# Keeping the finished tiles of two graph convolutions on chip and storing them behind the pass

## What is computed

```python
def _gcn_conv(x, W, b, src, dst, norm, num_nodes):
    h = x @ W
    msg = norm[:, None] * h[src]
    agg = jax.ops.segment_sum(msg, dst, num_segments=num_nodes)
    return agg + b
...
h = jax.nn.relu(_gcn_conv(x, W1, b1, src2, dst2, norm, N))
h = jax.nn.relu(_gcn_conv(h, W2, b2, src2, dst2, norm, N))
return h @ Wfc + bfc
...
x = _layernorm(x + _L0_gnn_ref(...))
# the start of the attention layer
x = (x - mu) * jax.lax.rsqrt(var + LN_EPS) * ln_gamma + ln_beta
x = x @ W_in + b_in
scores_u = x @ W_u + b_u
scores_v = x @ W_v
```

## Time and profile before

| | |
|---|---|
| median of 3 runs | 7572.42 us (7566.16 to 7602.41) |
| the profiled execution | 7592.25 us, its span 7590.4 us |
| mean granted TensorE clock | 0.769 of full speed |
| busy share of the span | PE 65%, VectorE 62%, ScalarE 42%, POOL 65% |
| DMA | 925.17 MB, mean 122 GB/s |
| pass c1 | gathers from 1327.36 to 2392.48 us, next stage's first gather at 2417.78 |
| pass c2 | gathers from 2417.78 to 3481.83 us, next stage's first gather at 3550.20 |

### The profile page before, as it was taken

One profiled execution on the slowest core, in us unless ns is written; L12 is line 12 of the kernel. 1 busy time (PEld: TensorE's weight loads), 2 busy tenths in 40 slices (PEclk: granted clock), 3 DMA queues, 4 the chain that ended last, 5 costly groups with the idle time before them and its releaser, 6 DMA issues. The chain is left out here.

```text
span 7590.4 us, 94731 instructions
## 1 busy us (share of the span) xinstructions
PE 4935.2 (65%) x26906; PEld 3772.5 (50%) x26906; DVE 4690.6 (62%) x12437; ACT 3186.4 (42%) x7393; POOL 4909.0 (65%) x4968
## 2 busy tenths in 40 slices
PE   8999701667676777774356655856656666777774
PEld 6777601444444555553344544435555543555553
DVE  8999701555554677775456666645666566566666
ACT  0222200444443444441244444735665642555553
POOL 0677775777776777774777773047777700777774
PEclk9767655888887888886566667967777777889887
DMA  1333201222223222223566665557777822666665
GB/s 29 80 81 79 58 2 28 53 56 55 55 55 48 53 55 56 56 56 65 162 179 178 178 178 120 194 189 231 232 224 223 224 66 79 217 211 207 208 211 146
DMA packets 793547, 925.17 MB, mean 122 GB/s; under 512 B 115987, under 2 KB 652059, under 8 KB 786139
## 3 DMA queue, kind: packets, MB, share of 16 engines
q0 software_dynamic: 198144, 441.54, 22.8%
q1 hardware_dynamic: 372654, 365.42, 16.2%
q10 hardware_dynamic: 222252, 112.14, 5.0%
HBM read 724.85 MB, written 193.87 MB: 121 GB/s over the span
## 5 line engine op out<-in xcount | busy, mean ns | idle before, releaser
L757 POOL DMA_INDIRECT arena<-t,d_src x2496 | 2454.7, 983 | 908.2 <-issue 756.2
L796 PE MATMUL ps<-arena 128*128 128x128 f32 (+2 forms) x8320 | 1796.5, 377 | 699.2 <-DMA arena<-t,d_src 616.4
L796 PEld LDWEIGHTS ps<-arena 128*128 128x128 f32 x8320 | 1584.7, 257 | 951.9 <-issue 845.9
L805 DVE TENSOR_TENSOR arena<-arena,ps 128x512 f32 (+2 forms) x1040 | 835.1, 803 | 733.8 <-PE ps L796 661.8
L757 POOL DMA_INDIRECT arena<-t,d_typed x832 | 823.9, 990 | 489.0 <-issue 248.3
L721 POOL DMA_INDIRECT d_rec<-arena x784 | 792.6, 1011 | 441.5 <-issue 250.3
L2749 POOL DMA_INDIRECT arena<-t,s_dst x832 | 797.4, 958 | 296.0 <-issue 249.6
L793 PE MATMUL ps<-int_tmp 128*128 128x512 bf16 (+1 forms) x1664 | 555.3, 402 | 488.1 <-DVE arena L805 305.1
L1973 PE MATMUL ps<-arena 128*128 x2496 | 420.2, 303 | 544.3 <-ACT arena L1869 255.8
L1234 PE MATMUL ps<-arena 128*128 128x416 f16 x3328 | 760.5, 382 | 0.0
L1973 PEld LDWEIGHTS ps<-arena 128*128 128x128 f32 (+1 forms) x2496 | 363.9, 210 | 611.5 <-issue 587.2
(11 more groups left out here) (451 smaller groups left out, 8079.8 us busy)
## 6 DMA issues: line engine op xcount, KB each, us to landing
spill<-arena ACTq DMA_DIRECT2D x104, 1024.0 KB, 7.5
arena<-spill SPq DMA_DIRECT2D x208, 512.0 KB
arena<-d_loT SPq DMA_DIRECT2D x104, 512.0 KB
arena<-s_loT SPq DMA_DIRECT2D x52, 1024.0 KB, 6.0
arena<-key_d SPq DMA_DIRECT2D x98, 512.0 KB
t<-arena SPq DMA_DIRECT2D x49, 1024.0 KB, 4.5
arena<-t,d_src POOLq DMA_INDIRECT x2496
arena<-t,d_typed POOLq DMA_INDIRECT x832
```

The lines of the kernel that those rows point to most:

```text
L757: pool.indirect_dma_start(out=rows[r][:, i, :], out_offset=None, in_=table, in_offset=bass.IndirectOffsetOnAxis(ap=idx[:, 8 * n + i:8 * n ...
L796: return nc.tensor.matmul(self.banks[i // 4][:, bass.ds(self.slot[i], self.width)], weights, rows, start=False, stop=False, skip_group_che ...
L805: nc.vector.tensor_tensor(at, at, got, ALU.add).then_inc(self.added, 1)
```

## The change

In both `sync` functions SP first waits until `added` has reached 204 of 208, and issues all stores behind that. In c2 the features are written into the tile's own columns of `acc_gcn` and the scores into an array of their own behind it, so there is no row block to wait for, and each tile is stored by two DMAs, 512 bytes and 32 bytes a row.

```diff
@@ FirstNodes.sync @@
+                sp.wait_ge(self.sums.added, 2 * HALVES - 4)
                 for t in range(0, DONE):
                     sp.wait_ge(self.out, t + 1)
                     store(t)
@@ SecondNodes.__init__ @@
-                for n in [REST * D] * 7 + [REST * (D + H), NT * H] + [REST * 6] * 2 + [REST * 2] * 2 + [REST] * 6:
+                for n in [REST * D] * 7 + [0, NT * H] + [REST * 6] * 2 + [REST * 2] * 2 + [REST] * 6:
...
-                self.rows = rows.rearrange("p (t f) -> p t f", f=D + H)
+                self.scores = arena[:, AT_ACC + NP:AT_ACC + NP + NT * H]
@@ SecondNodes.feature_rows @@
                 step = Chain(dve, self.y_v, t)
-                need(dve, self.stored, 16 * t)
-                step(nc.vector.tensor_tensor(self.rows[:, 0:w, 0:D], tiled(self.vectors_bank(1, w)), bcast_mid(bias["L1_gnn_b_in"], w), ALU.add))
+                step(nc.vector.tensor_tensor(tiled(of_tiles(acc_gcn, t, w)), tiled(self.vectors_bank(1, w)), bcast_mid(bias["L1_gnn_b_in"], w), ALU.add))
@@ SecondNodes.score_rows @@
-                step(nc.vector.tensor_tensor(self.rows[:, 0:w, D:D + H], uv[:, :, 0:H], bcast_mid(b_u[:, :], w), ALU.add))
+                step(nc.vector.tensor_tensor(tiled(of_tiles(self.scores, t, w, H), H), uv[:, :, 0:H], bcast_mid(b_u[:, :], w), ALU.add))
@@ SecondNodes.sync @@
-                def store(t, i):
+                def store(t):
                     number, = numbers(sp, t, 1)
-                    sp.dma_start(t2[bass.ds(P * number, P), :], self.rows[:, i, :]).then_inc(self.stored, 16)
+                    sp.dma_start(t2[bass.ds(P * number, P), 0:D], of_tiles(acc_gcn, t)).then_inc(self.stored, 16)
+                    sp.dma_start(t2[bass.ds(P * number, P), D:D + H], of_tiles(self.scores, t, 1, H)).then_inc(self.stored, 16)
+                sp.wait_ge(self.sums.added, 2 * HALVES - 4)
                 for t in range(0, DONE):
                     sp.wait_ge(self.rows_rdy, 2 * t + 2)
-                    store(t, 0)
+                    store(t)
                 sp.wait_ge(self.rows_rdy, 2 * DONE + 2)
-                for i in range(REST):
-                    store(DONE + i, i)
+                for t in range(DONE, NT):
+                    store(t)
...
-                sp.wait_ge(self.stored, 16 * NT)
+                sp.wait_ge(self.stored, 32 * NT)
```

More of the change, by code:

```diff
@@ L1331, in __init__ @@
                 assert o <= REP_AT
-                self.A, self.aT, self.hT, self.r, self.z, self.zT, self.xiT, rows, self.v_new = buf[0:9]
-                self.rows = rows.rearrange("p (t f) -> p t f", f=D + H)
+                self.A, self.aT, self.hT, self.r, self.z, self.zT, self.xiT, _, self.v_new = buf[0:9]
+                self.scores = arena[:, AT_ACC + NP:AT_ACC + NP + NT * H]
+                assert AT_ACC + NP + NT * H <= AT_Q
                 self.parts = [a.rearrange("p (t c) -> p t c", c=6) for a in buf[9:11]]
```

## The result

| | before | after |
|---|---|---|
| median of 13 runs | 7576.53 us (7565.63 to 7602.41) | 7590.32 us (7581.34 to 7596.07) |
| ratio, 95% interval | | 1.0018 [1.0011, 1.0025] |
| span of the profiled execution | 7590.4 us | 7588.4 us |
| c1, first gather to c2's first gather | 1090.4 us | 1103.2 us |
| c2, first gather to the next stage's first gather | 1132.4 us | 1138.2 us |

The changed kernel takes 13.8 us more, 0.18%. The two spans alone would say the opposite: the profiled execution of before lies 16 us above its median, and its stages behind c2, which the change does not touch, are 18.4 us longer than in the profile after.

What follows compares the result with a forecast made beforehand. POOL's gather issue was taken to pace both passes, and SP's stores to end c1. Terms -1.0 + 7.7 + 3 + 3.3 + 2.1 gave +15.1 us on the 7572.4 median: 7587.5 us, range 7562 to 7608.

Steps and rivals of the forecast that it cites:

- Stores leaving the pass: Mid-pass: taking the stores out gains nothing, since POOL's own issue sets the pace; 0 us.
- Rival 1: Mid-pass: the stores did slow the gathers, 10.6 ns each, 15.3 us saved in all, total 7572; chance 0.12.
- SP's stream in c1, +7.7: End of c1: 49 stores at 0.823 us each put the last at 2422.4 instead of 2414.67; +7.7 us.
- SP held by its queue, +3: End of c1: from about the 14th store SP is held behind slow gathers; +3 us, bounds 0 and 12.5.
- Rival 2: Ends of c1 and c2: queue stands still behind slow gathers, all upper bounds together +28.7 us, total 7601; chance 0.17.
- Turns between queues: DMA engines alternate queues by packet, so a store starts within one gather's packet; the sum would lack 3 us.
- Rival 3: Pass ends: stores take turns with the gathers and SP is never held; +12.1 us, total 7584.5; chance 0.15.
- The last gathers behind the stores: Pass ends: stores ahead of last gathers delay them; 2.8 us hidden in c1, +3.3 in c2, bounds 0 and 7.4.
- VectorE's wait, -1.0: Tail of c2: VectorE no longer waits for `stored`, which ended an idle time once; -1.0 us.
- The last four tiles of c2, +2.1: Behind c2: four tiles cost 1.35 us each instead of 0.823 ahead of the `s_loT` DMAs; +2.1 us.
- Slack ahead of the last four, 8.8: End of c2: 45 tiles are stored by 3533.3, the last four ready at 3542.1; 8.8 us to cover SP's holds.
- Rival 4: End of c2: 32-byte-row DMAs are slow, at 1.60 us each 43.6 us more, total 7631; chance 0.05.

Runs made afterwards that it cites:

- e9: Changed kernel's postponed stores in c1 only, c2 as in the kernel before; ratio to before 1.0013, c1's pause 38.09 us.
- e10: Changed kernel with c1's stores left in the pass, so only c2's are postponed; ratio to before 1.0005, c2's pause 70.87 us.
- e7: Changed kernel with SP waiting for all 208 sums in both passes, so no store runs beside a gather; ratio to before 1.0070.
- e11: Changed kernel with every second of c1's 45 postponed stores issued by ScalarE's queue; ratio to before 1.0008, c1's pause 26.81 us.
- e8: Changed kernel with SP's wait two steps earlier, at 200 of 208 sums, in both passes; ratio to before 1.0015.
- e5: Kernel before with filler records' source and typed index counting up instead of all zero; 7522.54 us against 7575.81, ratio 0.9928.

## Why the prediction was right, step by step

The forecast was +15.1 us and the total 7587.5; the measured total is 7590.3 and the difference 13.8, with an interval of 8 to 19. The two pauses together grew by 17.3 us, in e9 and e10 by 15.3. The mechanism was right, in that SP's stream and not the gathers ends c1; of the terms of the sum some were too large and some too small.

- **Stores leaving the pass, 0.** Shown: POOL's step is 1.280 us with and without them. Rival 1 had put the 10 ns between the first 96 gathers and the rest down to the stores; they are still there without stores (1.268 and 1.280 us in the changed kernel), so that they come from something else.
- **SP's stream in c1, +7.7.** Shown by e7, where it stands alone, and by e11, where halving it takes the pause back to 26.8. The stream was 1.0 us longer than 48 x 0.823, by the few wider steps.
- **SP held by its queue, +3.** Measured: the 14th store's issue took 2.74 us and the 22nd's 1.36, together 3.4 over two normal ones. That it was the 14th, as worked out from the earlier trace rows, is in part luck: three had landed by then, so ten stood in the queue, where the estimate has 14 there with none through. In e9 it was the 12th and 13th store that were held first, in e8, which starts ahead of the slow gathers, the 39th. In c2 a DMA is held for 0.8 to 1.4 us as early as the 2nd to 5th (changed kernel, e10, e11); with so few DMAs issued, the queue's length does not explain these, and their cause is open. In e7, without slow gathers beside it, nothing is held. Rival 2, the queue standing still for 12.5 us, did not come.
- **Turns between queues.** Stores landed up to 14.3 us behind their issue beside slow gathers, and 2.0 at most without (e7). By the Trainium skill (DMA: Bandwidth & Descriptors, Queues, rings and completion order) each DMA engine takes turns between the queues packet by packet. Once the stores run, e8's packets fit that: both queues move in the same 24 us, and neither waits for the other to empty. What the prediction drew from it, that a store starts within one gather's packet, is not so: the first store of the changed kernel sent nothing for 8.3 us while no gather's packet took over 2 us. Why it starts so late is open. Rival 3 falls with its consequence: stores issued every 0.83 us pile up when about one a us or fewer gets through, and SP was held in e9 and e8 too.
- **The last gathers behind the stores, 2.8 (hidden) and +3.3.** Too large: 1.6 us in c1 and 2.1 in c2; 1.4 in e9 and 1.8 in e10. In c2 the price accounts for it: the 32-byte rows were priced like 512-byte ones, but their packets took 9 ns where the others took 27, so that a pair of stores is 0.32 us of the engines, not 0.48, and 6.9 pairs are 2.2 us. In c1 the stores' packets ahead of the last gather's data are 2.5 us of the engines, and 1.6 arrive. e8 shows it larger, 4.3 of 8.4. Why not all of it arrives was not tried, and without any store beside them the last products of c1 lie between 10.99 and 11.82 us, so the small shares are uncertain.
- **VectorE's wait, -1.0.** The row is gone (`feature_rows` waits for no DMA any more), but the chain from the last sums to the last tile took 43.6 us in the changed kernel and 43.4 in e7, against 43.5 before; in e10 it took 42.3, in e9, where c2 is as before, 44.2. So it gave nothing that can be told from this spread.
- **The last four tiles of c2, +2.1.** Measured 2.5, from 8.1 us to 10.6 between the last tile ready and the next gather; the last two DMAs are 0.85 us apart instead of 0.53.
- **Slack ahead of the last four, 8.8.** It was 5.4: SP's eight held issues in c2 add 4.9 us, hidden in it.
- **Small rows slow.** Rival 4 falls: in c2 of the changed kernel tiles follow each other at 1.35 us as worked out, and at the median a small store lands 1.4 us behind its issue and a large one 1.6. The read-modify-write of rows under 512 bytes that the Trainium skill names (DMA: Bandwidth & Descriptors, its opening table) shows in none of these durations.

The errors had both signs. c1's pause cost 12.6 us where 10.7 was forecast; SP's stream and its holds together account for 1.5 of the 1.9 more. c2's cost 4.6 where 4.4 was, but that is luck: the landing and the wait's gain were both over, in opposite directions, and the same code cost 2.5 in e10 and 2.0 in e11. The total came within 1.3 us of the forecast although the pauses alone say 2.2 more; the run-to-run spread makes that closeness luck as well.

## What to carry to other kernels

The stores inside a pass that POOL paced cost nothing, and the same stores behind the pass cost what their queue needed to issue them: 49 at 0.83 us each are 40 us of work for SP, of which 12.6 stuck out here. If stores must be postponed, two queues (a pause of 26.8 us in e11) or a start early enough that most are out before the work that ends the pass (29.6 in e8) left less of it than the changed kernel's 37.9; neither came below the 25.3 of the kernel before. And look at what fillers fetch: some 20 gathers of one and the same row cost each of the five passes 10 to 19 us.

## What the runs showed of the hardware that was not expected

- An indirect gather whose 128 rows are all one table row takes the DMA engines seven times as long: 97.7% against 13.1% of 30 us for the same 1.18 MB (before and e5).
- A hardware queue with a backlog holds the engine that issues: in c1 at the 12th to 14th store issued beside the slow gathers, with some ten not yet landed, for up to 2.74 us, and ScalarE's queue as well as SP's (e11).
- The first store issued into a backlog of gathers sends its first packet 8.3 us later (changed kernel; 8.6 for the store at 3475.65 us in the kernel before), and yet both queues move together once stores run (e8).
- The program ran at 8881 us on one chip and at 7573 to 7577 on others, DMA packets and the time of a gather's issue (0.945 us) being the same. There TensorE paused up to 2.2 us between matmuls of one run of instructions, with nothing in the profile to wait for, and its granted clock was 0.72 in 1600 to 2300 us, against 0.83. What it waits for is open.
